# Linear attention's query pass: the squares of the queries move from ScalarE to VectorE

## The reference, cut to what matters

```
def softmax_kernel_features(data, proj, is_query):
    data_dash = einsum('bhnd,md->bhnm', data_normalizer * data, proj)
    diag_data = sum(square(data), -1) * 0.5 * data_normalizer ** 2
    stab = max(data_dash, -1) if is_query else max(data_dash)
    return ratio * (exp(data_dash - diag_data - stab) + EPS)
q1 = features(q, True);  k1 = features(k, False)
kv = einsum('bhnm,bhnd->bhmd', k1, v);  ksum = sum(k1, 2)
out = einsum('bhnm,bhmd->bhnd', q1, kv) / einsum('bhnm,bhm->bhn', q1, ksum)
h = h + out @ W_proj + b_proj
```

## Time and profile before

| | before |
|---|---|
| median of 3 runs | 2316.39 us |
| the profiled execution, its own time | 2327.7 us |
| span of its trace | 2325.6 us |
| TensorE matmul busy | 1849.9 us (80%) |
| VectorE busy | 1322.2 us (57%) |
| ScalarE busy | 1062.5 us (46%) |
| mean granted TensorE clock | 0.842 |

### The profile page before, as it was taken

The page is one execution under the profiler, slowest core; times in us unless marked ns, Lnnn a source line. Parts: engine busy times, 40 slices in busy tenths (PEclk is TensorE's granted clock), DMA queues, the critical chain, the costliest instruction groups (busy, mean ns, idle before and its releaser), DMA issues. The chain is left out here.

```text
span 2325.6 us, 30730 instructions
## 1 busy us (share of the span) xinstructions
PE 1849.9 (80%) x9722; PEld 998.1 (43%) x9746; DVE 1322.2 (57%) x2400; ACT 1062.5 (46%) x1948; POOL 561.9 (24%) x708
## 2 busy tenths in 40 slices
PE   3869878886866654777758877999899993999998
PEld 2745655453522431000012225444133332888887
DVE  3546336665511477999948886999844553122121
ACT  1102312222300375999969985333187771222221
POOL 5000000000021104766500002333004434233333
PEclk8979889996987675555569987998599996999999
DMA  3011110005599204334211116888686743677774
GB/s 87 1 43 32 42 39 19 18 12 208 199 408 409 106 1 131 98 101 130 66 34 40 31 26 97 124 127 125 77 92 96 99 103 105 198 199 201 211 203 108
DMA packets 153120, 258.49 MB, mean 111 GB/s; under 512 B 28560, under 2 KB 124673, under 8 KB 148006
## 3 DMA queue, kind: packets, MB, share of 16 engines
q1 hardware_dynamic: 134822, 239.15, 39.0%
q0 software_dynamic: 18176, 17.80, 4.0%
HBM read 215.16 MB, written 57.51 MB: 117 GB/s over the span
## 5 line engine op out<-in xcount | busy, mean ns | idle before, releaser
L1741 PE MATMUL ps<-arena 128*128 x376 | 194.8, 621 | 86.0 <-ACT ps L1824 64.8
L1824 ACT ACTIVATE ps<-ps,arena 128x512 f32<-128x512 f32 x384 | 256.1, 726 | 9.1 <-POOL arena L1805 9.1
L1751 DVE TENSOR_REDUCE arena<-ps 128x1024 f32 x192 | 232.8, 1224 | 28.9 <-PE ps L1741 16.0
L2193 DVE TENSOR_REDUCE arena<-ps 128x1024 f32 x192 | 221.1, 1215 | 11.1 <-PE ps L2439 8.7
L2662 ACT ACTIVATE arena<-ps 128x1024 f32<-128x1024 f32 x192 | 185.7, 1022 | 91.0 <-PE ps L2540 89.8
L2999 ACT ACTIVATE arena<-ps,arena 128x256 f32<-128x256 f32 x234 | 89.7, 482 | 235.8 <-PE ps L2964 235.8
L1983 ACT ACTIVATE arena<-ps 128x1024 f32<-128x1024 f32 x192 | 178.9, 1043 | 10.0 <-PE ps L1936 5.1
L2439 PE MATMUL ps<-arena 96*128 96x512 bf16 x500 | 163.8, 433 | 23.9 <-DVE arena L2193 11.3
L531 PE MATMUL ps<-arena 96*128 96x456 f32 (+1 forms) x512 | 176.3, 498 | 6.2 <-DMA arena<-la_xt 5.0
L2934 POOL DMA_INDIRECT out_dram<-arena x78 | 121.2, 1554 | 236.9 <-DVE arena L3023 165.8
L3019 DVE TENSOR_TENSOR arena<-ps,arena 128x384 f32<-128x384 f32 x39 | 21.8, 558 | 257.4 <-PE ps L2975 257.4
(11 more groups left out here) (393 smaller groups left out, 3214.9 us busy)
## 6 DMA issues: line engine op xcount, KB each, us to landing
arena<-in_sm_w_dram SPq DMA_DIRECT2D x128, 576.0 KB, 16.5
arena<-in_re_w_dram SPq DMA_DIRECT2D x39, 1252.0 KB, 5.8
arena<-ra_parts SPq DMA_DIRECT2D x192, 192.0 KB, 9.6
routed_in<-routed_in SPq DMA_DIRECT2D x8, 3332.0 KB, 13.9
ra_parts<-arena SPq DMA_DIRECT2D x48, 192.0 KB, 2.4
arena<-routed_in SPq DMA_DIRECT2D x39, 196.0 KB, 5.4
arena<-la_xt SPq DMA_DIRECT2D x16, 384.0 KB, 3.4
arena<-arena SPq DMA_DIRECT2D x64, 96.0 KB, 2.2
```

The source lines that it names most:

```text
L1741: ins = pe.matmul(ps[:, 2 * (n % 4) + t % 2, :], QM[j][:, h, t * P:(t + 1) * P], KI[:, b, h // HG, :], start=True, stop=True)
L1751: v.tensor_reduce(MXq[:, b, 2 * u:2 * u + 2, at_head(h)], ps[:, 2 * (n % 4):2 * (n % 4) + 2, :], AX.X, ALU.max).then_inc(s_lk, 1)
L1824: ins = act.activation(bank, bank, ACT.Exp, bias=nb[n % 4][:, t % 2:t % 2 + 1], scale=c_reg, accum_out=RS[:, b, t, at_head(h):at_head(h) + 1])
L2193: v.tensor_reduce(MX[:, bass.ds(b, 1), 2 * (n % 2):2 * (n % 2) + 2, n // 2].rearrange("p o t -> p (o t)"), ps[:, 2 * (n % 2):2 * (n % 2) + ...
```

## The change

In the query pass ScalarE no longer squares. VectorE waits for the products itself, copies the 192 query columns from PSUM to `SQ`, takes the maximum, multiplies `SQ` by the PSUM columns, and goes on as before; the maximum and the product are now linked, so the chain has four links in place of two. The semaphore `qsq` is gone. ScalarE's list is the exponential of tile t and the copy of tile t - 1 in a single loop over the batches. The key pass keeps `squares`.

```
@@ VectorE, chain
-                qsq.wait(v, b, t + 1)
-                v.tensor_reduce(mq[j].rearrange(...), features(t), AX.X, ALU.max)
+                qp.wait(v, b, t + 1)
+                q = ps[:, 2 * j, 0:D]
+                v.tensor_copy(SQ[j], q)
+                link(v.tensor_reduce(mq[j].rearrange(...), features(t), AX.X, ALU.max))
+                link(v.tensor_tensor(SQ[j], SQ[j], q, ALU.mult))
                 squared_lengths(v, link, t)
@@ VectorE, batch
-                link = Link(v, s_qk, b * (2 * T))
+                link = Link(v, s_qk, b * (4 * T))
@@ ScalarE, batch
                 for t in range(T + 1):
-                    if t < T - 1:
-                        squares(act, b, t + 1, qp, qsq)
-                    elif t == T - 1 and ahead:
-                        squares(act, b + 1, 0, qp, qsq)
                     if t < T:
                         qd.wait(act, b, t + 1)
                         act.activation(QD[t % 2], QD[t % 2], ACT.Exp).then_inc(qe.sem, 1)
                     if t:
                         qt.wait(act, b, t)
                         act.activation(Q1T[j]..., ps[0:2 * NF, 4:6, 0:3 * P]..., ACT.Identity, ...)
```

More of the change, by code:

```diff
@@ L788, in linear_attention @@
     SUMS, RD, TN, OT = g4(P, [S]), g4(P, [S // 32, 2]), g4(P, [S]), g4(P, [2, S])
-    qp, qsq, qd, qe, qt, qc = S1("q_products", T, T + 1), S1("q_squared", T), S1("q_features", T, 2), \
-        S1("q_exp", T, 2), S1("q_turned", T, 2), S1("q_turned_copied", T, 2)
+    qp, qd, qe, qt, qc = S1("q_products", T, T + 1), S1("q_features", T, 2), S1("q_exp", T, 2), \
+        S1("q_turned", T, 2), S1("q_turned_copied", T, 2)
     num, ot, pr, hh = S1("read_out", 2, 3), S1("normalised", 2), S1("projected"), S1("stream_updated")
@@ L815, in chain @@
                 j = t % 2
-                qsq.wait(v, b, t + 1)
-                v.tensor_reduce(mq[j].rearrange("p (g h) -> p g h", g=2), features(t), AX.X, ALU.max)
+                qp.wait(v, b, t + 1)
+                q = ps[:, 2 * j, 0:D]
+                v.tensor_copy(SQ[j], q)
+                link(v.tensor_reduce(mq[j].rearrange("p (g h) -> p g h", g=2), features(t), AX.X, ALU.max))
+                link(v.tensor_tensor(SQ[j], SQ[j], q, ALU.mult))
                 squared_lengths(v, link, t)
@@ L869, in _ @@
         def _(act):
-            for s in (qsq, qe, qc):
+            for s in (qe, qc):
                 s.start(act)
-            def batch(b, i, j, ahead):
-                prev(act, num, i, j)
-                for t in range(T + 1):
-                    if t < T - 1:
-                        squares(act, b, t + 1, qp, qsq)
-                    elif t == T - 1 and ahead:
-                        squares(act, b + 1, 0, qp, qsq)
[L880 to L890, removed]
-                for j in range(2):
-                    batch(2 * i + j, i, j, True)
-            batch(B - 2, B // 2 - 1, 0, True)
-            batch(B - 1, B // 2 - 1, 1, False)
+            with act.Fori(0, B // 2) as i:
+                for j in range(2):
+                    b = 2 * i + j
+                    prev(act, num, i, j)
+                    for t in range(T + 1):
+                        if t < T:
+                            qd.wait(act, b, t + 1)
+                            act.activation(QD[t % 2], QD[t % 2], ACT.Exp).then_inc(qe.sem, 1)
+                        if t:
+                            qt.wait(act, b, t)
+                            act.activation(Q1T[j][:, :, (t - 1) * P:t * P].rearrange("p (g a) q -> p g a q", g=2),
+                                           ps[0:2 * NF, 4:6, 0:3 * P].rearrange("p g (a q) -> p g a q", a=3),
+                                           ACT.Identity, bias=little[0:2 * NF]).then_inc(qc.sem, 1)
         @block.tensor
```

## The result

The changed kernel took 2278.64 us (median of 4 runs, 2276.47 to 2284.59) against 2314.72 for the kernel before: a ratio of 0.9855, 95% interval 0.9824 to 0.9886, so 26 to 41 us less. Run again later beside other kernels it had a ratio of 0.9881 (0.9858 to 0.9904), 22 to 33 us less. The prediction was 2288 us, that is 28.5 us less.

A forecast was written before the change was run, and what follows sets the result against it. TensorE and ScalarE waiting for each other in turn were taken to bound the query pass. 22.5 us of stalls plus 6 us of clock, 28.5 us, came off the 2316.4 us median: 2288 us, range 2281 to 2295.

The forecast's parts named there:

- The stalls come from ScalarE's list order: Query pass: ready exponential and copy stand behind a square needing the next products, stalling TensorE 2 x 1.83 us per batch.
- Stalls left in the pass: TensorE's waits before turn in the query pass: 31.2 us falls to 8.7, saving 22.5 us at full clock.
- Steady batch 19.84 us: Query pass loop at full clock: VectorE's 19.3 us of work plus two short waits sets the batch, against TensorE's 19.14.
- Copy and multiply at 358 ns: VectorE's two added operations per tile: 358 ns assumed for each, with 246 and 417 ns as ends.
- A link costs 0.12 us: VectorE's chain: each semaphore link between operations costs 0.12 us, where the Trainium skill's rule says nothing.
- The clock: TensorE in the loop: about half of the slow spells, worth about 11 us, go, saving 6 us.
- rival 1: Every slow spell inside the loop goes: 22.5 + 11 = 33.5 us saved, 2283 us; chance 0.17.
- outer range: Whole kernel: 2274 to 2302 us, with the 10 us spread of the earlier runs added to both ends.
- Rival 2: VectorE's two new operations cost 0.6 us each: batch 21.3 us, saving 15 with some clock, 2301 us; chance 0.12.
- Rival 3: Denser TensorE work in the loop draws more slow spells, 1.6 us each; with three per batch 2332 us; chance 0.03.
- Rival 4: Turn still starts late behind the copy, half the stall stays: saving about 9 to 11 us, 2306 us; chance 0.06.

The follow-up runs named there:

- e_order: Kernel before, with ScalarE's square of tile t+1 moved from in front of the exponential to behind the copy of tile t-1; ratio to before 0.9863, steady batch 19.55 us.
- e_wait: Changed kernel, with ScalarE again waiting for the next tile's products before each exponential but squaring nothing; ratio to before 0.9981, pass 212.2 us.
- e_nosq: Changed kernel without VectorE's copy, multiply and their two links, sums taken over ones; ratio to before 0.9824, steady batch 18.89 us.
- e_copy2: Changed kernel with VectorE's copy made twice per tile, the second into an unread tile; ratio to before 0.9896, steady batch 20.76 us.
- e_link: Changed kernel, with the multiply waiting only for VectorE's copy, no longer for the maximum directly in front; 2276.23 us, ratio to before 0.9843, steady batch 19.58 us.
- e_lists: Kernel before, with the square behind exponential and copy, and read_out, project and second normalise moved earlier in TensorE's and VectorE's lists; 2265.82 us, ratio to before 0.9803.

## Why the prediction was right, point by point

- **The stalls come from ScalarE's list order.** Shown, by taking the order away (e_order) and by giving the wait back (e_wait).
- **Stalls left in the pass: 8.7 us, a saving of 22.5.** Measured: 6.1 before turn and 2.2 more before project, 8.3 us; 22.9 us of idle went. No wait before turn above 0.4 us is left in the steady batches.
- **Steady batch 19.84 us, VectorE's list as the limit.** Measured 19.96; e_nosq and e_copy2 show VectorE as the limit. TensorE's own work was put at 19.14 us, it is 18.89: products in front of a turn take 2.42 us (409.52 to 411.94) from start to start, not 2.51; the two short waits were put at 0.52 and 0.18, they are 0.39 and 0.35.
- **Copy and multiply at 358 ns.** Measured 0.32 to 0.36 us.
- **A link costs 0.12 us.** e_link: 0.62 against 0.72 between the same two starts.
- **The clock: half of the slow spells go, 6 us.** This term was too small where it was meant, in the loop. All slow spells of the steady batches went, as the first rival had it. The pass by stretches, before and after: up to the first add 57.5 and 44.4 us, five steady batches 119.4 and 99.9, the batch behind them 22.5 and 22.4, the last from add to add 19.0 and 20.7, the end 2.1 and 2.1. Of the 31.0 us 22.9 are idle time of TensorE, and the other 8.1 I put down to clock; they were not measured apart from this difference. By the same differences the steady batches have 5.2 of clock and the stretch in front of them 5.3, together about rival 1's 11 us. The last two stretches lost some 2.5 again: their granted clock was 0.86 and 0.50 in the changed kernel and 0.92 and 0.67 in the one before, though their stalls are nearly the same. The changed kernel showed this slow end in both of its executions, and e_order in one of two, so it doesn't belong to the change alone.
- **The total.** The saving in the medians was 36.1 us in the first comparison and 27.4 in the second, around the 31.0 us of the pass. 2278.64 us lies in the outer range (2274 to 2302) but below the forecast's own (2281 to 2295), nearest to rival 1's 2283. The mechanism and the idle term are borne out; that the forecast's 28.5 us come so near to 31.0 is in part luck, since a clock term that was too small met a slower drain that I had not foreseen.
- **Rival 2 (VectorE binds harder)**: VectorE does bind, as in the forecast itself, but at 0.27 and 0.39 us from start to start for the two new operations and not at 0.6, so the batch is 19.96 and not 21.3 us. **Rival 3 (denser work draws slow spells)** is refuted by the opposite: TensorE busy without a gap had the full clock (e_nosq, e_lists). **Rival 4** (the copy still late) left 0.35 us in place of half a stall.

## What to carry to other kernels

An engine that is busy for a third of the time can hold up everything if its list has an operation that waits for new data in front of operations whose data are ready. Look at the idle time right before the stalled engine's releaser, and ask what each engine's next instruction was waiting for, not how busy it is. Before moving work to another engine try moving it within its list: here this gave more than the move across engines (19.55 against 19.96 us a batch), because it left the other engine its slack (VectorE busy for 15.4 against 18.15 us of it).

## What the runs showed of the hardware

- The granted clock in the loop of the pass. Kernels with two stalls of 1.6 to 1.8 us per batch (the kernel before and e_wait) had 5 slow batches of 10, each 1.5 to 1.7 us longer; with one of 1.7 us 2 of 10; with two of 1.2 to 1.3 us none of 10; the kernels with no stall above 0.9 us (the change, e_order, e_lists, e_link, e_nosq, e_copy2) had none in 40. What sets one off, the length of a stall or the idle time in all, stays open.
- Between two VectorE operations a wait for the one directly in front cost about 0.1 us, a wait for the one before that cost nothing that the rows show (0.62 us from maximum to multiply in e_link, and 0.63 behind the maximum without any link in the kernel before).
